# Half as many queries and two key tiles per step in an attention loop on eight cores

## The reference

```python
xn = layernorm(x)                                  # x: 4 x 4096 x 1024
Q, K, V = (xn @ W.T).reshape(16, 4, 4096, 64)      # for Wq, Wk, Wv: a plain reshape
out = softmax(Q @ K.T) @ V                         # no scale, no mask
y = out.reshape(4, 4096, 1024) + xn
attn = (y - mean(y)) / sqrt(var(y) + eps)          # over a whole batch element
ffn = sum over 8 experts of gate_e * ((xn @ w_in[e].T) @ w_out[e].T)   # top 2 gates
result = x + attn + ffn
```

## Time and profile before

| | before |
|---|---|
| median of three runs | 5671.61 us |
| lowest and highest of the three | 5669.56, 5804.27 us |
| profiled execution | 5671.61 us |
| its span on the slowest core | 5669.8 us |
| TensorE busy with matmuls | 4751.1 us (84%) |
| ScalarE busy | 2390.3 us (42%) |
| VectorE busy | 1391.5 us (25%) |
| mean granted TensorE clock | 0.876 |

### The profile page before, as it was taken

The page is one execution under the profiler, slowest core; times in us unless marked ns, Lnnn a source line. Parts: engine busy times, 40 slices in busy tenths (PEclk is TensorE's granted clock), DMA queues, the critical chain, the costliest instruction groups (busy, mean ns, idle before and its releaser), DMA issues.

```text
span 5669.8 us, 59428 instructions; the slowest of 8 cores (5653.1 to 5669.8 us)
## 1 busy us (share of the span) xinstructions
PE 4751.1 (84%) x19844; PEld 1721.1 (30%) x19844; DVE 1391.5 (25%) x3688; ACT 2390.3 (42%) x2275; POOL 146.9 (3%) x290
## 2 busy tenths in 40 slices
PE   1888888888888985888888888888959999999994
PEld 0422222222222113222222222222114444444442
DVE  4221211212112015121111211111033344444345
ACT  1456666566665542656666565665520000000000
POOL 1000000000000000000000000000000000000000
PEclk9989999898998556989899898996559999999997
DMA  5000000000000002000000000000037655567643
GB/s 77 6 1 4 4 1 4 2 3 4 1 4 4 1 2 32 1 5 1 4 4 1 4 1 4 4 1 0 1 60 119 95 87 93 91 111 119 106 76 85
DMA packets 86049, 173.72 MB, mean 31 GB/s; under 512 B 4864, under 2 KB 4864, under 8 KB 85760
## 3 DMA queue, kind: packets, MB, share of 16 engines
q0 software_dynamic: 83456, 161.54, 17.8%
q1 hardware_dynamic: 2304, 8.39, 0.4%
HBM read 323.06 MB, written 8.39 MB: 58 GB/s over the span
## 4 chain that ended last, share of the span: by engine, by line
PE 67%; ACT 15%; issue 6%; DVE 5%; DMA 4%; DVEq 2%; ACTq 1%; POOL 0%; POOLq 0%
PE P_OT L364 17%; PE P_S L421 17%; ACT AR L294 14%; PE P_S L497 13%; PE P_A L338 5%; PE P_B L338 5%; PE P_OT L515 4%; DMA AR<-woutT 3%; PE P_B L515 2%; PE P_A L515 2%; DMA xstg<-xb 1%; DVEq L612 1%; DVE gsc L613 1%; ACT AR L304 1%; PE P_A L347 1%
## 5 line engine op out<-in xcount | busy, mean ns | idle before, releaser
L294 ACT ACTIVATE AR<-P_S,consts 128x1024 bf16<-128x1024 f32 x2048 | 2261.4, 1116 | 1535.0 <-PE P_S L421 1532.1
L364 PE MATMUL P_OT<-AR 128*65 128x512 bf16 x4096 | 1408.0, 429 | 288.9 <-ACT AR L294 288.8
L421 PE MATMUL P_S<-AR 64*128 64x512 bf16 x4096 | 1415.9, 434 | 6.3 <-DVE AR L540 3.2
L497 PE MATMUL P_S<-AR 128*128 128x512 bf16 x4096 | 894.1, 381 | 17.8 <-DMA AR<-woutT 11.0
L364 PEld LDWEIGHTS P_OT<-AR 128*65 128x65 bf16 x4096 | 309.5, 115 | 1225.6 <-issue 1213.1
L497 PEld LDWEIGHTS P_S<-AR 128*128 128x128 bf16 x4096 | 401.9, 98 | 508.3 <-issue 31.8
L421 PEld LDWEIGHTS P_S<-AR 64*128 64x128 bf16 x4096 | 244.6, 98 | 974.8 <-issue 968.7
L724 DVE TENSOR_TENSOR AR<-P_S,AR 128x512 bf16<-128x512 f32 x384 | 265.7, 692 | 412.4 <-PE P_S L497 412.4
L531 DVE CAST AR<-P_B 64x256 bf16<-64x256 f32 x256 | 106.6, 417 | 984.9 <-PE P_B L338 984.9
L531 DVE CAST AR<-P_A 64x256 bf16<-64x256 f32 x256 | 106.6, 416 | 950.4 <-PE P_A L338 950.4
L338 PE MATMUL P_A<-xnTb,AR 128*64 128x256 bf16 x2048 | 297.0, 293 | 1.4 <-DVE xnTb L579 1.4
(11 more groups left out here) (98 smaller groups left out, 1618.7 us busy)
## 6 DMA issues: line engine op xcount, KB each, us to landing
AR<-winN POOLq DMA_DIRECT2D x64, 1024.0 KB, 14.6
AR<-woutT POOLq DMA_DIRECT2D x64, 1024.0 KB, 23.4
xstg<-xb POOLq DMA_DIRECT2D x80, 256.0 KB, 4.8
out<-AR SPq DMA_DIRECT2D x16, 512.0 KB, 2.9
AR<-wqT POOLq DMA_DIRECT2D x2, 1024.0 KB, 13.6
AR<-wkT POOLq DMA_DIRECT2D x2, 1024.0 KB, 25.2
AR<-wvT POOLq DMA_DIRECT2D x2, 1024.0 KB, 35.8
identsb<-idin POOLq DMA_DIRECT2D x1, 32.0 KB, 2.2
```

What stands on the lines that cost most here:

```text
L294: inst = ac.activation(AR[:, R_PT + sl * 1024: R_PT + (sl + 1) * 1024], stb[:, 0:1024], AF.Exp, bias=consts[:, 0:1])
L364: last = pe.matmul(pOT[0:65, hq * 512:(hq + 1) * 512], lhs, rhs, start=(k == 0), stop=(k == 31))
L421: last = pe.matmul(stb[0:128, hq * 512:(hq + 1) * 512], lhs, rhs, start=True, stop=True)
L497: last = pe.matmul(BK[bk][:, 0:512], lhs, rhs, start=(kt == 0), stop=(kt == 7))
```

## The change

Only attention is changed, its chunks and steps:

- A chunk has 512 queries, and a block has 8 chunks. A chunk still covers 32 key tiles, but in 16 steps of two tiles.
- A score matmul fills one bank: key tile `k` goes to bank `k % 4` of S0a, S0b, S0c, S0d, now one PSUM tensor of 2048 columns. TensorE issues scores 0 to 3, then for each pair an optional group, AV `k` and `k + 1`, scores `k + 4` and `k + 5`.
- One exp covers two neighbouring banks, that is the same 512 queries against two key tiles. It waits for both score matmuls and for the AV matmuls of two pairs earlier.
- An AV matmul adds into one bank: OTa in even chunks, OTb in odd ones.
- The copy at the end of a chunk is 65 x 512, into the half of `R_OUTS` that belongs to the chunk's parity. Four transposes follow in place of eight.
- The 36 groups are dealt as 5, 5, 5, 5, 5, 5, 5, 1 over the chunks, at `k` = 2, 8, 14, 20, 26, always ahead of the AV matmuls.
- The order of banks A and B and the names of labels are adapted.

```diff
-BANKS4 = ("S0a", "S0b", "S1a", "S1b")
+BANKS4 = ("S0a", "S0b", "S0c", "S0d")
+DEAL_CNT = (5, 5, 5, 5, 5, 5, 5, 1)
+DEAL_SLOTS = (2, 8, 14, 20, 26)
...
-                for qc in range(4):
-                    for k in range(32):
-                        gk = (pj * 4 + qc) * 32 + k
+                for qc in range(8):
+                    for k in range(0, 32, 2):
                         W(ac, ("st", pj, qc, k))
...
+                        W(ac, ("st", pj, qc, k + 1))
+                        pv = _eprev(pj, qc, k, 2)
+                        if pv is not None and pv[0] >= 8 * half:
+                            W(ac, ("av", pv[0], pv[1], pv[2] + 1))
+                        sl4 = k % 4
                         inst = ac.activation(
...
+                            AR[:, R_PT + ((k // 2) % 2) * 1024:
+                               R_PT + ((k // 2) % 2 + 1) * 1024],
+                            pS0[:, sl4 * 512: (sl4 + 2) * 512],
+                            AF.Exp, bias=consts[:, 0:1])
                         inc(inst, "sAC", ("exp", pj, qc, k))
                     W(ac, ("av", pj, qc, 31))
-                    if qc == 0 and pj > 0:
+                    if qc <= 1 and pj > 0:
                         W(ac, ("statsacc", pj - 1, 1))
-                    if qc > 0:
-                        W(ac, ("atr", pj, qc - 1, 7))
+                    if qc > 1:
+                        W(ac, ("atr", pj, qc - 2, 3))
                     ac.drain()
-                    inc(ac.copy(AR[0:65, R_OUTS: R_OUTS + 1024],
-                                pOT[0:65, 0:1024]), "sAC", ("outse", pj, qc))
+                    inc(ac.copy(AR[0:65, R_OUTS + (qc % 2) * 512:
+                                   R_OUTS + (qc % 2) * 512 + 512],
+                                pOT[0:65, (qc % 2) * 512:
+                                    (qc % 2) * 512 + 512]),
+                        "sAC", ("outse", pj, qc))
...
-                for qc in range(4):
+                for qc in range(8):
                     dealt = 0
-                    st_step(pj, qc, 0)
-                    st_step(pj, qc, 1)
-                    for k in range(32):
-                        if dealt < 9 and bgi < len(bg) and k % 3 == 1:
+                    for k in range(4):
+                        st_step(pj, qc, k, True)
+                    for k in range(0, 32, 2):
+                        if dealt < DEAL_CNT[qc] and bgi < len(bg) \
+                                and k in DEAL_SLOTS:
                             pe_qkv_group(*bg[bgi])
                             bgi += 1
                             dealt += 1
+                        W(pe, ("exp", pj, qc, k))
                         av_step(pj, qc, k)
-                        if k + 2 < 32:
-                            st_step(pj, qc, k + 2, _bacq=False)
-                    for jb in range(8):
+                        av_step(pj, qc, k + 1)
+                        for kk in (k + 4, k + 5):
+                            if kk < 32:
+                                st_step(pj, qc, kk, False)
+                    for jb in range(4):
                         bk = BANKOF[("atr", pj, qc, jb)]
                         bacq(pe, bk)
                         if jb == 0:
                             W(pe, ("outse", pj, qc))
...
-        P_S0 = _st.enter_context(nc.psum_tensor("P_S0", [128, 1024], F32))
-        P_S1 = _st.enter_context(nc.psum_tensor("P_S1", [128, 1024], F32))
+        P_S0 = _st.enter_context(nc.psum_tensor("P_S0", [128, 2048], F32))
```

More of the change, by code:

```diff
@@ L73, in _ab_schedule @@
         for pj in range(first, first + 8):
-            for qc in range(4):
+            gbase = 0
+            for qc in range(8):
                 if pj < first + 7:
-                    for g in range(9 * qc, 9 * qc + 9):
+                    for g in range(gbase, gbase + DEAL_CNT[qc]):
                         seq.append(("qkvg", pj + 1, g))
-                for jb in range(8):
+                gbase += DEAL_CNT[qc]
+                for jb in range(4):
                     seq.append(("atr", pj, qc, jb))
@@ L281, in emit_act, with _eprev @@
         ac.wait_ge(S["sGP"], 1)
+        def _eprev(pj, qc, k, back):
+            gk = ((pj * 8 + qc) * 32 + k) // 2 - back
+            if gk < 0:
+                return None
+            return (gk // 128, (gk // 16) % 8, (gk % 16) * 2)
         for half in range(2):
@@ L352, in av_step @@
         def av_step(pj, qc, k):
-            sl = k % 2
             par = pj % 2
-            W(pe, ("exp", pj, qc, k))
+            ot = "OTa" if qc % 2 == 0 else "OTb"
             if k == 0:
[L357 to L365, removed]
+                bacq(pe, ot)
+            lhs = AR[:, R_VB[par] + k * 65: R_VB[par] + k * 65 + 65]
+            rhs = AR[:, R_PT + ((k // 2) % 2) * 1024 + (k % 2) * 512:
+                     R_PT + ((k // 2) % 2) * 1024 + (k % 2) * 512 + 512]
+            last = pe.matmul(pOT[0:65, (qc % 2) * 512: (qc % 2) * 512 + 512],
+                             lhs, rhs, start=(k == 0), stop=(k == 31))
             inc(last, "sPE", ("av", pj, qc, k))
             if k == 31:
-                brel("OTa", ("outse", pj, qc))
-                brel("OTb", ("outse", pj, qc))
+                brel(ot, ("outse", pj, qc))
         def pe_phase0(seq0):
@@ L403, in emit_pe, with st_step @@
                 bgi = 0
[L405 to L411, removed]
-                    par = pj % 2
[L413 to L423, removed]
+                def st_step(pj, qc, k, explicit_wait):
+                    sl4 = k % 4
+                    sb = BANKS4[sl4]
+                    if explicit_wait:
+                        bacq(pe, sb)
+                    par = pj % 2
+                    lhs = AR[0:64, R_KT[par] + (k // 2) * 256
+                             + (k % 2) * 128:
+                             R_KT[par] + (k // 2) * 256 + (k % 2) * 128
+                             + 128]
+                    rhs = AR[0:64, R_QT[par] + qc * 512:
+                             R_QT[par] + qc * 512 + 512]
+                    last = pe.matmul(BK[sb][0:128, 0:512], lhs, rhs,
+                                     start=True, stop=True)
@@ L424, in st_step @@
                     inc(last, "sPE", ("st", pj, qc, k))
-                    brel(sb[0], ("exp", pj, qc, k))
-                    brel(sb[1], ("exp", pj, qc, k))
-                for qc in range(4):
+                    brel(sb, ("exp", pj, qc, k - (k % 2)))
+                for qc in range(8):
                     dealt = 0
-                    st_step(pj, qc, 0)
-                    st_step(pj, qc, 1)
-                    for k in range(32):
-                        if dealt < 9 and bgi < len(bg) and k % 3 == 1:
+                    for k in range(4):
[3 more added lines that the diff above has]
+                                and k in DEAL_SLOTS:
@@ L444, in emit_pe @@
                             W(pe, ("outse", pj, qc))
[L445 to L446 removed]
+                        src = AR[0:65, R_OUTS + (qc % 2) * 512 + jb * 128:
+                                 R_OUTS + (qc % 2) * 512 + (jb + 1) * 128]
                         inc(pe.transpose(BKBF[bk][:, 0:65], src,
@@ L602, in emit_dve @@
                         ALU.add, ALU.mult), "sDV", ("xnat", pj, th))
-                for qc in range(4):
+                gbase = 0
+                for qc in range(8):
                     if pj < first + 7:
-                        for gg in range(9 * qc, 9 * qc + 9):
-                            dve_qkv_evac(pj + 1, gg)
-                    for jb in range(8):
+                        for gg in range(gbase, gbase + DEAL_CNT[qc]):
+                            if gg < 36:
+                                dve_qkv_evac(pj + 1, gg)
+                    gbase += DEAL_CNT[qc]
+                    for jb in range(4):
                         W(dv, ("atr", pj, qc, jb))
                         bkn = BANKOF[("atr", pj, qc, jb)]
-                        gq = qc * 4 + jb // 2
+                        gq = qc * 2 + jb // 2
                         hb = jb % 2
```

19 lines of the change are left out of this document (6 added, 13 removed).

## The result

The changed kernel is slower: 5824 to 5832 us against 5669 to 5676 us for the kernel before on the same chips, ratio 1.0275 with a 95% interval of 1.0263 to 1.0288. The profiled execution took 5831.04 us, 159 us more than that of before.

A forecast was written before the change was run, and what follows sets the result against it. Attention was taken as bound by TensorE and ScalarE alternating, with serial chunk boundaries costing idle time, then low clock. 5671.6 us plus 248 for fourteen blocks and 12 for the halves' last blocks gave 5932 us, range 5835 to 6085.

The forecast's parts named there:

- The key step costs nothing: Attention steps: two key tiles against 512 queries cost the same as one against 1024; 128 steps per block both ways.
- The boundaries stay serial: Chunk ends: transposes still precede the next scores; each boundary shrinks from 7.53 to 4.64 us, chunks per block double to 8.
- The clock falls in the shorter gap: TensorE at chunk boundaries: the gap shrinks from 5.67 to 2.78 us, yet the clock falls at every new boundary.
- Rival B: Chunk boundaries: the clock survives the short gap, head 5.3 us, chunk 28.4 us, total 5388 us; chance 0.08.
- The head stays at 8.43 us: Chunk start, first scores to exp number 3: runs at the low clock and keeps its old length of 8.43 us.
- Chunks 0 to 5: Blocks with projection: boundary 4.64, head 8.43 and four cycles of 4.615 make 31.53 us each, 189.2 together.
- chunk 6: Blocks with projection: groups 30 to 34, three of them V groups adding 2.16 us, make 33.7 us.
- Rival D: Added boundaries mostly hidden: low stretch 4 us shorter per chunk, 2 us of work regained, total 5708 us; chance 0.06.
- The eighth chunk: Chunk 7 of blocks with projection: one V group in the slow head adds 1.82 us; chunk 30.1 us.
- Sum: Blocks with projection: 253.0 against 235.3 us, times 14 is +248 us; with +12 us for last blocks, 5932 us.
- The last blocks: Last block of each half, low clock throughout: 71.3 us per two chunks, 1.5 us more; eight pairs, +12 us.
- The range: Total of 5835 to 6085 us, covering copy bounds, a clock return up to 1 us of work earlier, and a later return.

The follow-up runs named there:

- reordered kernel: Changed kernel with scores two pairs ahead across chunks and blocks, copy after the next chunk's first exp, transposes at its third and fourth pair: 4926 us, ratio 0.8652.
- filled kernel: Changed kernel with unused matmuls of the scores' shape put into TensorE's pauses: 5845 to 5868 us.
- runs with more turns: Changed kernel with five or eight transposes and evacuations per chunk in place of four: 5955 us and 6201 to 6230 us.
- eight turns: Changed kernel with eight transposes and evacuations per chunk in place of four, the last one repeated: 6201 to 6230 us.
- three turns: Changed kernel with three transposes and evacuations per chunk in place of four, a quarter of the queries left out: 5777 to 5780 us.
- the other deal: Changed kernel with the groups dealt 5, 5, 5, 5, 4, 4, 4, 4 over the chunks: 5865 to 5867 us.
- filled boundaries: Boundaries with unused matmuls in TensorE's pauses, in the changed kernel (5845 to 5868 us) and in the kernel before (5838 to 5839 us).
- reordered kernel of before: Kernel before with scores two steps ahead across chunks, copy after the next chunk's first exp, eight transposes bunched at its steps 5 and 6: 5487 to 5489 us.
- that of before with spread transposes: Kernel before, reordered the same way, with its eight transposes spread singly over steps 5 to 12 of the next chunk: 5154 us.

## Why the prediction was right and wrong

- **The key step costs nothing: right.** Exps and matmuls have their old durations, and a cycle is 4.61 us.
- **The boundaries stay serial: right.** 4.61 us against 4.64; the copy 0.58 against 0.61 us. The reordered kernel shows what removing them gives.
- **The clock falls in the shorter gap: right** (2.75 us, 0.69 in the slice 1007 to 1008). Rival B fell; its price was right where a chunk of the filled kernel did keep the clock, 28.5 us. The Trainium skill (page TensorE: Matmul & The Clock Gate, section Why this matters for your kernels) says that gaps between bursts of matmuls cost the clock. The trace agrees, but the gaps that it warns of are longer than this one of 2.75 us, behind which the clock fell in 55 of 56 chunks: here the measurement decides.
- **The head stays at 8.43 us: wrong, and this is the step that failed.** It was 7.56 us in the chunk shown and 7.6 in most. I took one head for a constant, though it holds the return of a clock that the kernel doesn't command. Chunks 0 to 5 came out 0.8 us shorter, 5.0 us per block, and chunk 6 0.9. The runs with more turns show why: at eight turns the low stretch is 10.2 us again and the mean head 8.3 us. Rival D had this mechanism, and its low stretch was nearly right: it said 4 us shorter, and 3.4 were found (6.8 against 10.2 us). Its price was not. Of the old stretch 2.4 us lay over the idle boundary on average, of the new one 0.4, so the clock came back only 1.7 us sooner after the first scores (6.4 against 8.1 us) and 0.8 to 0.9 us of work was regained in place of 2.
- **The eighth chunk: mis-sized.** I added 1.82 us for a V group at the low level to a whole slow head, 30.1 us. Its matmuls did take 3.53 us, but the clock was back by their end, so the pairs behind ran at the high level: 28.6 us.
- **Sum.** Block 245.8 instead of 253.0, times 14 is -101 us. The last blocks took 281.1 us in place of 285 each, -8 us. About +8 us lie outside of what I worked out. The mean clock was 0.864 and not 0.83: there are 116 low stretches where there were 62, nearly as many more as forecast, but those of the blocks last 6.8 us and not 10, and all together 1588 us and not 1978.
- **The range** allowed for a clock that returns up to 1 us of work earlier, and gave it about 100 us. With the eighth chunk on top the time came out 3 to 11 us below its edge.

**What stays open.** Shown is that the mean return of the clock moves by up to 1.7 us, that changes of the boundary's length or of the deal move it, and that the low stretch is 6.8 us behind the boundary of the changed kernel and 10.2 us behind that of eight turns, and behind most of the kernel before. What picks the moment in a given chunk isn't settled. The gap's length alone does not: three turns have a shorter gap and a later return than four. Nor does the number of groups in the chunk: with the other deal it was later in the chunks that kept five groups too (7.6 us on average). It isn't settled either why the clock still fell at filled boundaries.

## What to carry to other kernels

Halving a chunk doubles its serial ends; make the last work of one chunk overlap the first of the next before making chunks smaller, and spread what is moved there: bunched it cost 333 us more (5487 against 5154 us). Here the same layout went from 2.75% slower to 13.5% faster when copy and transposes were issued behind the next chunk's first steps, for which the alternating output halves were of use. When a stretch at low clock is a term of a sum, give it a range from several of its occurrences: a microsecond removed at a boundary returned between 0.6 and 1.9 us.

## What was not expected of the hardware

- In the last block of each half TensorE is busy without a pause inside a chunk at the low level, and in the changed kernel too (0.50 over 281 us); in the reordered kernel, which enters that block at the high level, it holds it for most of the block (0.95). The matmuls are the same, the order and the level at entry are not. A reordered kernel that enters the block at the high level need not keep it, though: that of before with spread transposes does so too, loses it behind the first chunk's copy, and doesn't get it back in the three chunks that follow (63 us each).
- A pause of little more than one microsecond can stand ahead of a fall of the clock, shorter than the gaps of the earlier trace rows: no matmul in the slice 1012 to 1013 of the reordered kernel of before, 0.52 in the next. With the transposes spread, 14 of 25 pauses of 1.15 us had no fall behind them.
- The low stretches at the boundaries come in few lengths: 6.8 us in all 55 chunks of the changed kernel, 10.2 us in all 55 with eight turns, one or the other with five.
- Taking work from a boundary gave 0.36 us for the first 0.62 us and 1.19 us for the second.
